# Relation stage of a four-layer graph network: three of four tiles turned by the transposing transfer, one of four by TensorE

## The chip, the core and the metric

The kernel runs on one core of a Trainium2 chip. A core has TensorE (PE: matrix products into PSUM, with its weight loads, PEld), VectorE (DVE), ScalarE (ACT), GpSimd (POOL) and SyncE (SP), which run in parallel, each through its own list of instructions in order, and meet at semaphores. DMAs are issued by SP, ACT and POOL and run on 16 shared DMA engines. The metric is the device time of one execution in microseconds.

## The reference

Four graph layers with a residual and a layer norm after each. The change lies in the last, a relational graph convolution followed by a plain one:

```python
def _graph_encoder(x, edge_index, edge_type, W_rel, W_root, b_rgcn, W_gcn, b_gcn):
    n = x.shape[0]
    src, dst = (edge_index[0], edge_index[1])
    ones = jnp.ones((src.shape[0],), dtype=x.dtype)
    seg = edge_type * n + dst
    agg = jax.ops.segment_sum(x[src], seg, num_segments=N_REL * n)
    cnt = jax.ops.segment_sum(ones, seg, num_segments=N_REL * n)
    mean = agg.reshape(N_REL, n, -1) / jnp.maximum(cnt, 1.0).reshape(N_REL, n, 1)
    h1 = jnp.einsum('rni,rio->no', mean, W_rel) + x @ W_root + b_rgcn
    ...
x = _layernorm(x + _L3_gnn_ref(x, edge_index, edge_type_34, ...), axis=-1)
```

There are 1250 nodes with 768 features, 20000 edges and 34 relations, each with its own 768 x 768 weights, all in 32-bit floating point.

## The kernel before

The layers run one after the other. In the relation stage the kernel doesn't form the means first. It has sorted the edges by relation and cut each relation's edges into tiles of 128, padded, `RT` = 190 tiles in all. For each tile it gathers the 128 source rows of x, multiplies them by the relation's weights, scales each row by the inverse count of its segment, and stores the messages to memory (`msg_d`). A later stage gathers and sums them by target node.

A product needs the tile turned: features on the partitions, edges along the row. There are two ways, and tiles with even and odd numbers take one each.

- **Turned by TensorE** (even tiles before). POOL gathers rows of `x3_d` into `rows7` (L1907). `turn` makes six transposes of 128 x 128 on TensorE into PSUM (L1936). `take` on ScalarE copies the result out of PSUM twice, plain into `xt7` (L1994) and rounded into `xhi7` (L1995).
- **Turned by a transfer** (odd tiles before; the code calls them crossed). POOL gathers rows of `x3p_d`, a copy of x in which each row is split in a plane of upper and one of lower 16-bit halves, into one of two buffers `halfs7`. `cross` on ScalarE's queue issues a transposing DMA from there into `plane7`, of which there is one (L1980). `take` puts the halves together into `xt7` (L1997) and rounds into `xhi7` (L1998).

After either, POOL subtracts the rounded from the plain values, `low` (L1913), so that the tile stands as a high and a low part. `messages` on TensorE is 36 matmuls (L1948): two halves of the 768 output columns, three products (high x high, high x low, low x high), six pieces of 128 features. Each tile's result takes two PSUM banks, and two tiles alternate. `store` on ScalarE scales the result into `msg7` (L2004) and issues its DMA (L2007). VectorE splits each relation's weights into high and low parts (L1880, L1881), and SyncE then loads the next relation's (L1873).

The order is written out by hand. For each tile k ScalarE does `store(k)`, then `take(k + 3)`, and after every second pair a `cross`. `store(k)` waits for the product of tile k, `take` for the turn or the transfer, and for `low` two tiles earlier. The product of tile k waits for `low(k)` and for `store(k - 2)`, which frees its PSUM. POOL issues the gather of an even tile when the one before it has been turned, and of a crossed tile when the transfer that read its buffer has landed; then it does `low(k)`.

Of the kernel before, what the change touches and what calls it, by code (L numbers as in the profile page):

```python
# [25 lines left out]
HALF = D // 2  # L26
# [3 lines left out]
RT = (E + R * (P - 1)) // P + 1  # L30
# [45 lines left out]
def build(nc, a, out):  # L76
    ctx = ExitStack()
    with ctx:
# [28 lines left out]
        ident = sb("ident", [P, P])  # L107
# [24 lines left out]
        ps = ctx.enter_context(nc.psum_tensor("ps", [P, 8, 512], F32))  # L132
# [25 lines left out]
        def halves(v):  # L158
            return v.rearrange("p (a n) -> p a n", a=2)
# [1725 lines left out]
        def dve_rel(v, step):  # L1885
# [12 lines left out]
                    relation(2 * i + 1 + u, 1 - u)  # L1898
            relation(R - 1, 1)

        def pool_rel(g, step):
            def gather(k):
                if k % 2 == 0 and k >= 2:
                    g.wait_ge(s_turn7, k // 2)
                if k % 2 == 1 and k >= 5:
                    g.wait_ge(s_cross7, 16 * ((k - 4) // 2 + 1))
                g.indirect_dma_start(out=rows7 if k % 2 == 0 else halfs7[:, k // 2 % 2, :], out_offset=None,  # L1907
                                     in_=x3_d if k % 2 == 0 else x3p_d,
                                     in_offset=bass.IndirectOffsetOnAxis(relrec[:, 2 * k:2 * k + 1], 0)).then_inc(s_gath[k % GW], 16)
# [6 lines left out]
            for k in (1, 0, 3):  # L1916
                gather(k)
            g.dma_start(rows8, row_d.rearrange("(p k) c -> p (k c)", p=P)).then_inc(s_idx8, 16)
            for k in range(RT):
                ahead = k + (2 if k % 2 == 0 else 4)  # L1920
                if ahead < RT:
                    gather(ahead)
                low(k)
            for u in range(GW):
                g.wait_ge(s_gath[u], 16 * len(range(u, RT, GW)))

        def pe_rel(pe):
            W_ROOT.multiply_resident(pe, lambda j: z6[:, j, :], lambda j: pe.wait_ge(s_ready6, j + 1))
            pe.sem_inc(s_prod7, 2)

            def turn(u, gathers, k):
                pe.wait_ge(s_gath[u % GW], 16 * gathers)
                if not isinstance(k, int) or k >= 4:
                    pe.wait_ge(s_take7, k - 3)
                for c in range(KC):
                    last = pe.transpose(ps[:, 2 * (u // 2 % 2) + c // 3, (c % 3) * P:(c % 3 + 1) * P], rows7[:, c * P:(c + 1) * P], ident[:, :])  # L1936
                last.then_inc(s_turn7, 1)

            def messages(k, u):
                r = pe.value_load(tile_rel[0:1, bass.ds(k, 1)], min_val=0, max_val=R - 1)  # L1940
                pe.wait_ge(s_split7, r + 2)
                base = (r % 2) * (KC * D)
                pe.wait_ge(s_lo7, k + 1)
                pe.wait_ge(s_emp7, k + 1)
                for h in range(2):
                    for q, (x, w) in enumerate(((xhi7, whi7), (xhi7, wlo7), (xlo7, whi7))):
                        for c in range(KC):
                            last = pe.matmul(ps[:, 4 + 2 * (u % 2) + h, 0:HALF], x[:, u, c * P:(c + 1) * P],  # L1948
                                             w[:, bass.ds(base + (c * D + h * HALF), HALF)],
                                             start=(q == 0 and c == 0), stop=(q == 2 and c == KC - 1))  # L1950
                last.then_inc(s_prod7, 1)

            turn(0, 1, 0)
            pe.wait_ge(W_ROOT.emptied, W_ROOT.b["emptied"] + NT + 2)
            turn(2, 1, 2)
            messages(0, 0)
            messages(1, 1)
            whole = (RT - 4) // XW
            with pe.Fori(0, whole) as i:
                for u in range(2, XW + 2):  # L1960
                    k = XW * i + u
                    if u % 2 == 0:
                        turn(u + 2, i + 1 + (u + 2) // XW, k + 2)
                    messages(k, u % XW)
            for k in range(whole * XW + 2, RT):
                if k % 2 == 0 and k + 2 < RT:
                    turn(k + 2, (k + 2) // XW + 1, k + 2)
                messages(k, k % XW)

        def act_rel(act, step):  # L1970
            act_root(act)
            act.wait_ge(W_ROOT.product, W_ROOT.all_products)

            def cross(u, gathers, taken=True):


                act.wait_ge(s_gath[u % GW], 16 * gathers)
                if taken:
                    act.sem_inc(s_take7, 1)
                act.dma_start_transpose(plane7.rearrange("p (c r) -> p c r", r=P), halfs7[:, u // 2 % 2, :]).then_inc(s_cross7, 16)  # L1980

            def take(k, u, turns):
                if u % 2 == 0:
                    act.wait_ge(s_turn7, turns)
# [6 lines left out]
                x = xt7[:, u % 2].rearrange("p c n -> p (c n)")  # L1991
                if u % 2 == 0:
                    pair = ps[:, 2 * (u // 2 % 2):2 * (u // 2 % 2) + 2, 0:HALF]
                    step.count(act.activation(halves(x), pair, ACT.Copy))  # L1994
                    step(act.activation(halves(xhi7[:, u % XW, :]), pair, ACT.Copy))  # L1995
                else:
                    step(act.activation(x.bitcast(U16).rearrange("p (n t) -> p t n", t=2), plane7.rearrange("p (t n) -> p t n", t=2), ACT.Copy))  # L1997
                    step(act.activation(xhi7[:, u % XW, :], x, ACT.Copy))  # L1998
                    act.sem_inc(s_take7, 1)  # L1999

            def store(k, u, stores):
                act.wait_ge(s_prod7, k + 3)
                act.wait_ge(s_msgst[u % 2], PLANES - 16 + 16 * stores)
                step(act.activation(halves(msg7[:, u % 2, :]), ps[:, 4 + 2 * (u % 2):6 + 2 * (u % 2), 0:HALF], ACT.Copy,  # L2004
                                    scale=invs[:, bass.ds(k, 1)]))
                act.sem_inc(s_emp7, 1)
                act.dma_start(msg_d[bass.ds(k * P, P), :], msg7[:, u % 2, :]).then_inc(s_msgst[u % 2], 16)  # L2007

            act.sem_inc(s_emp7, 2)
            cross(1, 1, taken=False)  # L2010
            take(0, 0, 1)
            act.sem_inc(s_take7, 1)
            take(1, 1, 1)
            take(2, 2, 2)
            cross(3, 1)
            store(0, 0, 1)
            take(3, 3, 2)
            store(1, 1, 1)
            take(4, 4, 3)
            cross(5, 2)  # L2020
            whole = (RT - 6) // XW
            with step.loop(whole, 3 * XW) as i:
                for u in range(XW):
                    k = XW * i + u + 2
                    store(k, u + 2, 2 * i + 1 + (u + 2) // 2)
# [3 lines left out]
            for k in range(whole * XW + 2, RT):  # L2029
                store(k, k, k // 2 + 1)  # L2030
                if k + 3 < RT:
                    take(k + 3, k + 3, (k + 3) // 2 + 1)
                    if k % 2 == 1:
                        cross(k + 4, (k + 4) // XW + 1)
            for u in range(2):
                act.wait_ge(s_msgst[u], PLANES - 16 + 16 * (RT // 2 + 1))


        UP = 4
# [216 lines left out]
```

## Time and profile before

| | us |
|---|---|
| median of 3 runs | 3793.22 (3791.40 to 3793.32) |
| the profiled execution, its own time | 3791.21 |
| its span in the profile | 3789.6 |
| mean granted clock of TensorE, share of full speed | 0.971 |

The span is what one profile shows from first to last instruction; the execution's own time lies 1.6 us above it. The relation stage's products run from 2074.8 to 3325.8 us, a third of the span. In the views, ACTq, POOLq and SPq are the queues in which ScalarE, POOL and SyncE issue DMAs; "idle before" is how long the engine did nothing before an instruction, and behind the arrow stands what ended it. The names of tiles are those of the buffers they are cut from: `ct` holds `rows7`, `halfs7`, `plane7`, `xt7` and `msg7`; `xsplit` holds `xhi7` and `xlo7`; `wsplit` the split weights; `ps` is PSUM.

### The profile page before, as it was taken

How to read it: one execution, taken by the hardware profiler on the slowest of the kernel's cores; microseconds unless marked ns; L12 is line 12 of the kernel's file. 1: busy time of each engine (PE TensorE's matmuls, PEld its weight loads, DVE VectorE, ACT ScalarE, POOL GpSimd, SP SyncE). 2: the span in 40 equal slices, each digit the busy share in tenths (PEclk: the TensorE clock that was granted, in tenths of full speed). 3: DMA queues.
4: the chain of work that ended last, by engine and by line, in shares of the span. 5: the costliest groups of instructions: out<-in, count | busy, mean ns of one | idle time of the engine just before them, and what ended most of it. 6: DMA issues, size and time to landing. Idle time of an engine off the chain costs nothing.

```text
span 3789.6 us, 56202 instructions
## 1 busy us (share of the span) xinstructions
PE 3509.1 (93%) x17647; PEld 2879.3 (76%) x17663; DVE 1956.8 (52%) x2740; ACT 1804.7 (48%) x2929; POOL 1751.0 (46%) x1329
## 2 busy tenths in 40 slices
PE   8998769999889897599989999999999999989998
PEld 4654449999789896233336999999999999955598
DVE  7537788888434545899955333333333331023335
ACT  1117878888633222599972444444444444400021
POOL 6888887765300001677101444444444444367600
PEclk9999979999989998899999999999999999999999
DMA  3321123333323213211025777777777775589801
GB/s 110 96 67 27 36 51 77 97 79 81 94 100 103 88 42 105 82 42 42 35 82 174 231 224 220 229 218 210 220 221 227 224 224 149 136 289 305 259 15 67
DMA packets 327199, 509.49 MB, mean 134 GB/s; under 512 B 195219, under 2 KB 211658, under 8 KB 327076
## 3 DMA queue, kind: packets, MB, share of 16 engines
q0 software_dynamic: 59584, 185.70, 16.9%
q1 hardware_dynamic: 85412, 194.37, 15.3%
q10 hardware_dynamic: 182080, 127.88, 12.0%
q8 instruction: 65, 1.06, 0.1%
q14 instruction: 58, 0.48, 0.0%
HBM read 346.22 MB, written 123.73 MB: 124 GB/s over the span
## 4 chain that ended last, share of the span: by engine, by line
PE 40%; ACT 7%; POOL 5%; issue 3%; DVE 2%; DMA 1%; SPq 0%; POOLq 0%; DVEq 0%; ACTq 0%
PE ps L1948 31%; POOL work L2055 5%; ACT work L1305 4%; ACT ps L1296 3%; PE ps L1588 3%; PE ps L307 2%; PE ps L1936 2%; PE ps L299 2%; DVE work L1127 1%; PE ps L1242 1%; DVE work L1155 0%; ACT work L1315 0%; DMA ct<-x_d 0%; DMA work<-msg_d,ct 0%; PE ps L325 0%
## 5 line engine op out<-in xcount | busy, mean ns | idle before, releaser
L1948 PE MATMUL ps<-wsplit,xsplit 128*128 x6840 | 1212.8, 336 | 0.0
L1948 PEld LDWEIGHTS ps<-wsplit,xsplit 128*128 128x128 f32 x6840 | 1185.0, 188 | 0.2 <-issue 0.2
L1913 POOL TENSOR_TENSOR xsplit<-ct,xsplit 128x768 fp32r<-128x768 f32 x190 | 361.4, 1902 | 368.6 <-ACTq L1999 240.8
L1305 ACT ACTIVATE work<-ps,work 128x418 f32<-128x418 f32 x720 | 438.4, 632 | 107.3 <-PE ps L1215 101.7
L1880 DVE CAST wsplit<-wplain 128x768 fp32r<-128x768 f32 x204 | 137.7, 675 | 680.1 <-PE ps L1948 659.2
L1252 PE MATMUL ps<-hbuf,work 128*128 128x193 f32 x2400 | 454.7, 327 | 16.2 <-DVE work L1169 13.1
L1252 PEld LDWEIGHTS ps<-hbuf,work 128*128 128x128 f32 x2400 | 407.0, 190 | 44.0 <-issue 16.7
L1296 ACT ACTIVATE ps<-work,lr 128x418 f32<-128x418 f32 x720 | 431.4, 633 | 6.4 <-DMA work<-lrow_d 6.4
L1155 DVE SCALAR_TENSOR_TENSOR work<-work,cnt 128x1250 f32<-128x1250 f32 x240 | 349.7, 1457 | 133.8 <-ACT work L1305 131.4
L2004 ACT ACTIVATE ct<-ps,invs 128x768 f32<-128x768 f32 x190 | 171.8, 904 | 485.7 <-PE ps L1948 472.6
L1242 PE MATMUL ps<-work,hbuf 128*65 128x512 f32 x720 | 323.4, 532 | 37.8 <-DVE work L1155 36.0
L299 PE MATMUL ps<-wsplit,xsplit 128*128 128x384 f32 x1800 | 336.7, 345 | 12.7 <-DVE xsplit L370 11.9
L299 PEld LDWEIGHTS ps<-wsplit,xsplit 128*128 128x128 f32 x1800 | 322.3, 195 | 15.0 <-issue 12.9
L801 POOL DMA_INDIRECT row_d<-hbuf x160 | 257.0, 1606 | 50.9 <-issue 48.5
L1215 PE MATMUL ps<-work 128*128 128x418 bf16 x720 | 247.4, 345 | 30.3 <-DMA work<-shift_d 25.9
L801 POOL DMA_INDIRECT relrec_d<-work x160 | 251.8, 1574 | 48.8 <-issue 48.5
L1349 POOL DMA_INDIRECT invs<-inv_d,relrec x190 | 219.6, 1156 | 117.5 <-issue 61.4
L2069 PE MATMUL ps<-work 128*128 128x384 f32 x784 | 257.2, 490 | 12.7 <-DMA work<-msg_d,ct 12.6
L1881 DVE TENSOR_TENSOR wsplit<-wplain,wsplit 128x768 fp32r<-128x768 f32 x204 | 253.8, 1244 | 7.1
L801 POOL DMA_INDIRECT dstrec_d<-work x160 | 216.7, 1354 | 66.5 <-issue 48.5
L2069 PEld LDWEIGHTS ps<-work 128*128 128x128 f32 x784 | 149.4, 191 | 120.1 <-issue 15.5
L1997 ACT ACTIVATE ct<-ct 128x1536 uint16<-128x1536 uint16 x95 | 186.1, 1959 | 111.8 <-DMA ct<-ct 65.8
(221 smaller groups left out, 4247.9 us busy)
## 6 DMA issues: line engine op xcount, KB each, us to landing
wplain<-in_L_gnn_W_rel SPq DMA_DIRECT2D x34, 2304.0 KB, 10.5
msg_d<-ct ACTq DMA_DIRECT2D x190, 384.0 KB, 2.6
work<-lrow_d SPq DMA_DIRECT2D x47, 625.0 KB, 3.9
feat_d<-work ACTq DMA_DIRECT2D x30, 386.0 KB, 2.6
hbuf<-feat_d SPq DMA_DIRECT2D x60, 193.0 KB, 2.5
gat_d<-work POOLq DMA_DIRECT2D x12, 960.0 KB, 5.3
xplain<-gat_d SPq DMA_DIRECT2D x30, 384.0 KB, 3.1
wplain<-x_d SPq DMA_DIRECT2D x20, 384.0 KB, 3.1
```

What stands on the lines that cost most here:

```text
L299: last = pe.matmul(ps[:, 4 + 2 * u + h, 0:HALF], x[:, u, c * P:(c + 1) * P], w[:, c * D + h * HALF:c * D + (h + 1) * HALF], start=(q == 0 ...
L801: g.indirect_dma_start(out=(dstrec_d, relrec_d, row_d)[which], out_offset=bass.IndirectOffsetOnAxis((addr[:, 1, t:t + 1], addr[:, 0, t:t + ...
L1155: v.scalar_tensor_tensor(p[:, 0:N], p[:, 0:N], 1.0, cnt3[:, q % NT, 0:N], ALU.min, ALU.mult).then_inc(self.s_p, 1)
L1215: pe.matmul(ps[:, b, 0:c1 - c0], self.ones128, self.crow[h % 2][:, c0:c1], start=False, stop=True, skip_group_check=True).then_inc(self.s_ ...
L1242: last = pe.matmul(ps[0:C + 1, 3 + k, 0:n1 - n0], self.feat(h, s), p[:, n0:n1], start=(s == 0), stop=(s == NT - 1))
L1252: last = pe.matmul(ps[:, self.b0 + b, t * (C + 1):(t + 1) * (C + 1)], p[:, dt * P:(dt + 1) * P], self.feat(h, s), start=(s == 0 and t == 0 ...
L1296: act.activation(ps[:, b, 0:c1 - c0], self.Rb[h % 2][:, c0:c1], ACT.Relu, bias=lr[:, col:col + 1]).then_inc(self.s_relu, 1)
L1305: act.activation(self.p[q % 3][:, c0:c1], ps[:, b, 0:c1 - c0], ACT.Exp, bias=self.l2[:, col:col + 1], scale=1.0 - SLOPE)\
L1881: step(v.tensor_tensor(wlo7[:, at:at + D], w, whi7[:, at:at + D].bitcast(F32), ALU.subtract))
L1913: g.tensor_tensor(xlo7[:, k % XW, :], xt7[:, k % 2].rearrange("p c n -> p (c n)"), xhi7[:, k % XW, :].bitcast(F32), ALU.subtract).then_inc ...
L1948: last = pe.matmul(ps[:, 4 + 2 * (u % 2) + h, 0:HALF], x[:, u, c * P:(c + 1) * P], w[:, bass.ds(base + (c * D + h * HALF), HALF)], start=( ...
L2069: last = pe.matmul(ps[:, 2 * (u % 2) + h, 0:HALF], sel8[:, GT * (u % 2) + w, :], mg8[:, GT * u + w, h * HALF:(h + 1) * HALF], start=(w == ...
```

## The change

Tiles with a number that four divides are turned by TensorE, all others by the transfer: 48 and 142 instead of 95 and 95. `crossed(k)` counts the crossed tiles below k, and so names the buffer of `halfs7` and the count of transfers to wait for. `cross` moves into `take`: as soon as a crossed tile is taken, the transfer for the next crossed tile is issued. ScalarE's loop body covers eight tiles instead of four. Turned tiles use one pair of PSUM banks instead of two in turn.

```diff
+        def by_transfer(k):
+            return k % XW != 0
+
+        def crossed(k):
+            return k - (k + XW - 1) // XW
+
+        def next_crossed(k):
+            return k + 1 if by_transfer(k + 1) else k + 2
...
             def gather(k):
-                if k % 2 == 0 and k >= 2:
-                    g.wait_ge(s_turn7, k // 2)
-                if k % 2 == 1 and k >= 5:
-                    g.wait_ge(s_cross7, 16 * ((k - 4) // 2 + 1))
-                g.indirect_dma_start(out=rows7 if k % 2 == 0 else halfs7[:, k // 2 % 2, :], out_offset=None,
-                                     in_=x3_d if k % 2 == 0 else x3p_d,
+                if by_transfer(k):
+                    if crossed(k) >= 2:
+                        g.wait_ge(s_cross7, 16 * (crossed(k) - 1))
+                    rows, source = halfs7[:, crossed(k) % 2, :], x3p_d
+                else:
+                    if k >= XW:
+                        g.wait_ge(s_turn7, k // XW)
+                    rows, source = rows7, x3_d
+                g.indirect_dma_start(out=rows, out_offset=None, in_=source,
...
-                ahead = k + (2 if k % 2 == 0 else 4)
+                ahead = next_crossed(next_crossed(k)) if by_transfer(k) else k + XW
...
-            turn(0, 1, 0)
+            turn(1, 0)
             pe.wait_ge(W_ROOT.emptied, W_ROOT.b["emptied"] + NT + 2)
-            turn(2, 1, 2)
-            messages(0, 0)
-            messages(1, 1)
+            for k in range(2):
+                messages(k, k)
             whole = (RT - 4) // XW
             with pe.Fori(0, whole) as i:
                 for u in range(2, XW + 2):
-                    k = XW * i + u
-                    if u % 2 == 0:
-                        turn(u + 2, i + 1 + (u + 2) // XW, k + 2)
-                    messages(k, u % XW)
+                    if u == 2:
+                        turn(i + 2, XW * i + XW)
+                    messages(XW * i + u, u % XW)
...
+            TURN = 2 * XW
...
-            def take(k, u, turns):
+            def take(i, c, more=True):
+                k = TURN * i + c
+                if by_transfer(c):
+                    act.wait_ge(s_cross7, 16 * (crossed(TURN) * i + crossed(c) + 1))
                 else:
-                    act.wait_ge(s_cross7, 16 * turns)
+                    act.wait_ge(s_turn7, 2 * i + c // XW + 1)
...
+                if by_transfer(c):
+                    step(act.activation(x.bitcast(U16).rearrange("p (n t) -> p t n", t=2), plane7.rearrange("p (t n) -> p t n", t=2), ACT.Copy))
+                    step(act.activation(xhi7[:, c % XW, :], x, ACT.Copy))
+                    if more:
+                        cross(i, next_crossed(c))
+                    else:
+                        act.sem_inc(s_take7, 1)
...
-                    take(k + 3, u + 5, 2 * i + (u + 5) // 2 + 1)
-                    if u % 2 == 1:
-                        cross(u + 6, i + (u + 6) // XW + 1)
+            whole = (RT - 6) // TURN - 1
+            with step.loop(whole, 3 * TURN) as i:
+                for c in range(2, TURN + 2):
+                    store(i, c)
+                    take(i, c + 3)
```

ScalarE's list before, just ahead of its loop, from the transfer for tile 3 to the transfer for tile 5. In brackets are the semaphores an instruction waits for: `product7` the product, `turned7` and `turned_by_transfer7` the two ways of turning, `rows_gathered` a gather, `act_step` ScalarE's own last instruction.

```order
L1980 DMA_TRANSPOSE ct<-ct 128x12x128 [waits act_step,rows_gathered3]
L2004 ACTIVATE ct<-ps,invs 128x768 [waits messages_stored0,product7]
L2007 DMA msg_d<-ct 128x768 [waits act_step]
L1997 ACTIVATE ct<-ct 128x2x768 [waits low_parts7,turned_by_transfer7]
L1998 ACTIVATE xsplit<-ct 128x768 [waits act_step]
L2004 ACTIVATE ct<-ps,invs 128x768 [waits act_step,messages_stored1,product7]
L2007 DMA msg_d<-ct 128x768 [waits act_step]
L1994 ACTIVATE ct<-ps 128x768 [waits product7,low_parts7,turned7]
L1995 ACTIVATE xsplit<-ps 128x768
L1980 DMA_TRANSPOSE ct<-ct 128x12x128 [waits act_step,rows_gathered1]
```

Between two transfers stand two stores and the takes of tile 3 and tile 4. ScalarE's list after, at the same place, from the transfer for tile 2 to the one for tile 5:

```order
L1993 DMA_TRANSPOSE ct<-ct 128x12x128 [waits act_step,rows_gathered2]
L2008 ACTIVATE ct<-ct 128x2x768 [waits low_parts7,turned_by_transfer7]
L2009 ACTIVATE xsplit<-ct 128x768 [waits act_step]
L1993 DMA_TRANSPOSE ct<-ct 128x12x128 [waits act_step,rows_gathered3]
L2024 ACTIVATE ct<-ps,invs 128x768 [waits messages_stored0,product7]
L2027 DMA msg_d<-ct 128x768 [waits act_step]
L2008 ACTIVATE ct<-ct 128x2x768 [waits low_parts7,turned_by_transfer7]
L2009 ACTIVATE xsplit<-ct 128x768 [waits act_step]
L1993 DMA_TRANSPOSE ct<-ct 128x12x128 [waits act_step,rows_gathered1]
```

A transfer now stands right behind each take of a crossed tile, and the next crossed tile's take waits for it with at most one store between. TensorE's list at the stage's start before: the turns (L1936) of tiles 0 and 2, then the first product's look-up of its relation.

```order
L307 MATMUL ps<-mask,ct 128x384 x24
L1936 MATMUL ps<-ident,ct 128x128 x12
L1940 TENSOR_LOAD tile_rel
L1940 ISA x2
L1941 REGISTER_ALU
```

The same place after, with `turn` now on L1949:

```order
L307 MATMUL ps<-mask,ct 128x384 x24
L1949 MATMUL ps<-ident,ct 128x128 x6
L1953 TENSOR_LOAD tile_rel
L1953 ISA x2
L1954 REGISTER_ALU
```

Tile 2's six transposes are gone from it.

## Rows read from the trace of the kernel before

**Rows 1.** The page: the span

```profile
span 3789.6 us, 56202 instructions
```

**Rows 2.** Chain of waits, 2500 to 2700 us: shares by line; start us, us, what

```profile
by line: PE ps L1948 95.2%; PE ps L1936 4.9%
...
2564.01 12.51 PE ps L1948 x72
2590.32 12.51 PE ps L1948 x72
```

**Rows 3.** Stretches: window, us, busy us of each engine, granted clock, DMA share, GB/s

```profile
3000.00:3200.00 200.00, 200.00 (x1187) 199.49 (x1186) 59.00 (x68) 92.84 (x92) 89.15 (x61) 1.00 0.68 198
```

**Rows 4.** Groups by line, 2100 to 3100 us: busy us, mean ns | idle before, releasers

```profile
L1997 ACT ACTIVATE ct<-ct 128x1536 uint16<-128x1536 uint16 x77 | 151.0, 1961 | 94.6 <-DMA ct<-ct 60.2 <-ACT ct L2004 34.4
L2004 ACT ACTIVATE ct<-ps,invs 128x768 f32<-128x768 f32 x152 | 137.4, 904 | 377.1 <-PE ps L1948 364.2 <-issue 7.6 <-ACT xsplit L1998 5.4
```

**Rows 5.** ScalarE's timeline: start us, us, engine, line, op [idle before, releaser]

```profile
2602.97 0.90 ACT L2004 ACTIVATE ct<-ps,invs 128x768 f32<-128x768 f32 x1 [1.53 <-PE ps L1948]
...
2604.67 0.82 ACT L1994 ACTIVATE ct<-ps 128x768 f32<-128x768 f32 x1 [0.80 <-ACT ct L2004]
2605.38 0.81 ACT L1995 ACTIVATE xsplit<-ps 128x768 fp32r<-128x768 f32 x1
2606.37 1.83 ACTq L1980 DMA_TRANSPOSE ct<-ct  x1
2609.95 0.90 ACT L2004 ACTIVATE ct<-ps,invs 128x768 f32<-128x768 f32 x1 [3.76 <-PE ps L1948]
2611.11 0.35 ACTq L2007 DMA_DIRECT2D msg_d<-ct  x1
2611.66 1.97 ACT L1997 ACTIVATE ct<-ct 128x1536 uint16<-128x1536 uint16 x1 [0.81 <-ACT ct L2004]
2613.67 0.85 ACT L1998 ACTIVATE xsplit<-ct 128x768 fp32r<-128x768 f32 x1
2616.11 0.90 ACT L2004 ACTIVATE ct<-ps,invs 128x768 f32<-128x768 f32 x1 [1.59 <-PE ps L1948]
...
2619.50 2.88 ACTq L1980 DMA_TRANSPOSE ct<-ct  x1
...
2626.71 1.95 ACT L1997 ACTIVATE ct<-ct 128x1536 uint16<-128x1536 uint16 x1 [2.66 <-DMA ct<-ct]
...
2629.88 0.90 ACT L2004 ACTIVATE ct<-ps,invs 128x768 f32<-128x768 f32 x1 [0.34 <-ACT xsplit L1998]
```

**Rows 6.** Timeline of all engines, same columns

```profile
2602.67 0.82 PE L1936 MATMUL ps<-ident,ct 128*128 128x128 f32 x6
...
2614.64 0.37 SPq L1873 DMA_DIRECT2D wplain<-in_L_gnn_W_rel  x1
```

**Rows 7.** Line L1980, 2100 to 3300 us: duration ns min/median/max, landing

```profile
L1980 ACTq DMA_TRANSPOSE ct<-ct x91: 1452/2032/4160, 2106.4 to 3290.5; - x91
...
DMA to landing us min/median/max: 3.7/4.3/8.2
```

**Rows 8.** DMA issues, 2100 to 3100 us: xcount, KB each, median us to landing

```profile
wplain<-in_L_gnn_W_rel SPq DMA_DIRECT2D x30, 2304.0 KB, 10.5
msg_d<-ct ACTq DMA_DIRECT2D x152, 384.0 KB, 2.6
...
ct<-x3p_d,relrec POOLq DMA_INDIRECT x76, 4.5
```

**Rows 9.** ScalarE's timeline at the stage's start

```profile
2076.68 5.49 ACTq L1980 DMA_TRANSPOSE ct<-ct  x1
...
2087.53 1.98 ACT L1997 ACTIVATE ct<-ct 128x1536 uint16<-128x1536 uint16 x1 [3.12 <-DMA ct<-ct]
```

**Rows 10.** TensorE's timeline near 3600 us

```profile
3600.58 6.24 PE L299 MATMUL ps<-wsplit,xsplit 128*128 128x384 f32 x24 [2.23 <-DVE xsplit L370]
```

**Rows 11.** Stretches: the columns of rows 3, after that wait

```profile
3601.80:3605.20 3.40, 3.37 (x11) 3.31 (x11) 3.04 (x4) 0.00 (x0) 0.00 (x0) 0.51 0.06 25
```

More of the change, by code:

```diff
@@ L1914, in low @@
                                 ALU.subtract).then_inc(s_lo7, 1)
-            for k in (1, 0, 3):
+            for k in (1, 0, 2):
                 gather(k)
@@ L1929, in pe_rel, with turn @@
             pe.sem_inc(s_prod7, 2)
[L1931 to L1934, printed above, removed]
+            def turn(gathers, k):
+                pe.wait_ge(s_gath[0], 16 * gathers)
+                if not isinstance(k, int) or k >= XW:
+                    pe.wait_ge(s_take7, k - XW + 1)
                 for c in range(KC):
-                    last = pe.transpose(ps[:, 2 * (u // 2 % 2) + c // 3, (c % 3) * P:(c % 3 + 1) * P], rows7[:, c * P:(c + 1) * P], ident[:, :])
+                    last = pe.transpose(ps[:, c // 3, (c % 3) * P:(c % 3 + 1) * P], rows7[:, c * P:(c + 1) * P], ident[:, :])
                 last.then_inc(s_turn7, 1)
@@ L1960, in pe_rel @@
                 for u in range(2, XW + 2):
-                    k = XW * i + u
-                    if u % 2 == 0:
-                        turn(u + 2, i + 1 + (u + 2) // XW, k + 2)
-                    messages(k, u % XW)
+                    if u == 2:
+                        turn(i + 2, XW * i + XW)
+                    messages(XW * i + u, u % XW)
             for k in range(whole * XW + 2, RT):
-                if k % 2 == 0 and k + 2 < RT:
-                    turn(k + 2, (k + 2) // XW + 1, k + 2)
+                if not by_transfer(k + 2) and k + 2 < RT:
+                    turn((k + 2) // XW + 1, k + 2)
                 messages(k, k % XW)
@@ L1972, in act_rel, with cross @@
             act.wait_ge(W_ROOT.product, W_ROOT.all_products)
-            def cross(u, gathers, taken=True):
-                act.wait_ge(s_gath[u % GW], 16 * gathers)
+            TURN = 2 * XW
+            def cross(i, c, taken=True):
+                act.wait_ge(s_gath[c % GW], 16 * (2 * i + c // XW + 1))
                 if taken:
                     act.sem_inc(s_take7, 1)
-                act.dma_start_transpose(plane7.rearrange("p (c r) -> p c r", r=P), halfs7[:, u // 2 % 2, :]).then_inc(s_cross7, 16)
-            def take(k, u, turns):
-                if u % 2 == 0:
-                    act.wait_ge(s_turn7, turns)
+                act.dma_start_transpose(plane7.rearrange("p (c r) -> p c r", r=P), halfs7[:, crossed(c) % 2, :]).then_inc(s_cross7, 16)
+            def take(i, c, more=True):
+                k = TURN * i + c
+                if by_transfer(c):
+                    act.wait_ge(s_cross7, 16 * (crossed(TURN) * i + crossed(c) + 1))
                 else:
-                    act.wait_ge(s_cross7, 16 * turns)
+                    act.wait_ge(s_turn7, 2 * i + c // XW + 1)
                 if not isinstance(k, int) or k >= 2:
@@ L1990, in take @@
                     act.wait_ge(s_prod7, k - 1)
[L1991 to L1993 removed]
+                x = xt7[:, c % 2].rearrange("p c n -> p (c n)")
+                if by_transfer(c):
[5 more added lines that the diff above has]
+                        act.sem_inc(s_take7, 1)
+                else:
+                    pair = ps[:, 0:2, 0:HALF]
@@ L1994, in take, with store @@
                     step.count(act.activation(halves(x), pair, ACT.Copy))
[L1995 to L1998, printed above, removed]
+                    step(act.activation(halves(xhi7[:, c % XW, :]), pair, ACT.Copy))
                     act.sem_inc(s_take7, 1)
-            def store(k, u, stores):
+            def store(i, c):
+                k, u = TURN * i + c, c % 2
@@ L2002, in store @@
                 act.wait_ge(s_prod7, k + 3)
-                act.wait_ge(s_msgst[u % 2], PLANES - 16 + 16 * stores)
-                step(act.activation(halves(msg7[:, u % 2, :]), ps[:, 4 + 2 * (u % 2):6 + 2 * (u % 2), 0:HALF], ACT.Copy,
+                act.wait_ge(s_msgst[u], PLANES + 16 * ((TURN // 2) * i + c // 2))
+                step(act.activation(halves(msg7[:, u, :]), ps[:, 4 + 2 * u:6 + 2 * u, 0:HALF], ACT.Copy,
                                     scale=invs[:, bass.ds(k, 1)]))
                 act.sem_inc(s_emp7, 1)
-                act.dma_start(msg_d[bass.ds(k * P, P), :], msg7[:, u % 2, :]).then_inc(s_msgst[u % 2], 16)
+                act.dma_start(msg_d[bass.ds(k * P, P), :], msg7[:, u, :]).then_inc(s_msgst[u], 16)
@@ L2009, in act_rel @@
             act.sem_inc(s_emp7, 2)
[L2010 to L2025, printed above, removed]
-                    take(k + 3, u + 5, 2 * i + (u + 5) // 2 + 1)
-                    if u % 2 == 1:
-                        cross(u + 6, i + (u + 6) // XW + 1)
@@ L2029, in act_rel @@
-            for k in range(whole * XW + 2, RT):
-                store(k, k, k // 2 + 1)
+            cross(0, 1, taken=False)
+            for k in range(3):
+                take(0, k)
+            for k in range(2):
+                store(0, k)
+                take(0, k + 3)
+            whole = (RT - 6) // TURN - 1
[3 more added lines that the diff above has]
+                    take(i, c + 3)
+            for k in range(whole * TURN + 2, RT):
+                store(0, k)
@@ L2031, in act_rel @@
                 if k + 3 < RT:
-                    take(k + 3, k + 3, (k + 3) // 2 + 1)
-                    if k % 2 == 1:
-                        cross(k + 4, (k + 4) // XW + 1)
+                    take(0, k + 3, next_crossed(k + 3) < RT)
             for u in range(2):
-                act.wait_ge(s_msgst[u], PLANES - 16 + 16 * (RT // 2 + 1))
+                act.wait_ge(s_msgst[u], PLANES + 16 * (RT // 2))
         UP = 4
```

## Prediction

> **What bounds the kernel now.** I read the span first, 3789.6 us [rows 1], and then the chain of waits over the relation stage, where the change is. There the chain is TensorE (PE) alone: 95.2% message products (L1948) and 4.9% turns (L1936) [rows 2]. The table by stretches agrees: PE busy 200.00 of 200 us at granted clock 1.00, ScalarE (ACT) only 92.84 [rows 3]. So in this stage every microsecond off TensorE's list is one off the run, as long as nobody arrives late. Who could be late, the groups by line [rows 4] and ScalarE's timeline [rows 5, 6] tell: of 1000 us ScalarE waits 364.2 for a product to end, and 60.2 for a transposing transfer to land. That second wait is the one to watch.
>
> **What the change removes.** A message product is 36 matmuls. Four tiles take 26.31 us (2564.01 to 2590.32); their two pairs of products are 2 x 12.51 = 25.02 of it [rows 2]. The two turns between them cost the rest, 1.29, or 0.65 us each. (A turn's six transposes are busy for 0.82 us [rows 6], but overlap the products, so I take 0.65.) Of 190 tiles, 95 are turned on TensorE before and 48, every fourth, after: 47 x 0.65 = **-30.6 us**. TensorE's floor for four tiles becomes 25.02 + 0.65 = 25.67 us. This is the whole gain, and it needs the transfers to keep up.
>
> **What it adds.** 47 more transfers, and above all a new order: for three tiles of four ScalarE's list is store, take, transfer, and the next tile's take waits for exactly that transfer. There is one buffer for turned planes (`plane7`), so a transfer can't be issued before the take that empties it has ended. Before, a tile turned by TensorE lay between any two takes from `plane7`, and the transfer had that time. ScalarE's steps:
> - Store to the take after it, when nothing is waited for: 2609.95 to 2611.66, 1.71 us [rows 5].
> - A take from a transfer, up to the issue of the next: from 2611.66 to the end of the second ACTIVATE at 2614.52, and the 0.18 that lie between the end of L1995 (2606.19) and the issue at 2606.37: 3.04 us [rows 5].
> - The issue holds ScalarE's sequencer for a median of 2.03 us (1.45 to 4.16) [rows 7]; all that is queued behind it on ScalarE waits. About 0.3 more to the next store.
> - Issue to landing: median 4.3 us (3.7 to 8.2) [rows 7], and 0.2 to the take.
> - A take from TensorE's turn: 2604.67 to 2606.19, 1.52 us, and 0.34 to a store that follows a take at once (2629.88) [rows 5].
>
> From one transferred tile's take to the next: 3.04 + 4.5 = 7.5 us, where a tile's products are 12.51 / 2 = 6.25. ScalarE falls behind by 1.3 us at each of the two steps of a group that go from transfer to transfer. In the third the turned tile lies between, and the transfer is hidden: 3.04 + 2.03 + 0.3 + 1.71 + 1.52 + 0.34 + 1.71 = 10.7. A group of four: 2 x 7.5 + 10.7 = **25.7 us**, against TensorE's 25.67. Undisturbed, ScalarE just keeps pace (47 groups x 0.03, **+2**) and can catch nothing up. From the shortest values of [rows 7] the group is 2 x 6.9 + 10.1 = 23.9 and ScalarE gains 1.8 us in each; if every issue held it for 2.88, as the one at 2619.50 did, the steps would be 3.04 + 2.88 + 0.3 + 1.71 = 7.9 and the group 27.4, 1.7 us late each time (+80 us). I take the medians, since they come from 91 transfers.
>
> How late may ScalarE be? A store frees the PSUM that the product two tiles on writes. The one at 2609.95 is done at 2610.85. That product starts some 0.3 us before the store at 2616.11, as PE's turn at 2602.67 stands before the store at 2602.97: 2615.8 - 2610.9 = 4.9 us of cover [rows 5, 6]. Behind a late take on ScalarE stands the next store, for which TensorE waits, and POOL's low part with the gather after it.
>
> **The weight loads.** Every fifth tile, on average, SyncE loads 2304 KB, 10.5 us from issue to landing, 30 times in 1000 us [rows 8]. The transfer issued 4.9 us into such a load (2614.64, 2619.50) gave its take at 2626.71, 7.2 us later instead of 4.5, and ScalarE stood idle for it [rows 5, 6]: +2.7. Before, this lay inside the cover. Afterwards three transfers are issued in 25.7 us; if those issued in the first 7 us of a load are hit, a load meets 3 x 7 / 25.7 = 0.8 of them (an estimate), 25 in some 31 loads. One third is hidden behind the turned tile and costs only the longer hold, 2.88 - 2.03 = 0.85: 8 x 0.85 = 7. The others cost 2.7 each: 17 x 2.7 = 46. Together **+53 us**, and **-5** for the cover, which is used up once because nothing is caught up. Bounds: nothing (first rival), and 25 x 3.9 = 98 us with the longest landing, 8.2.
>
> **The start.** Tile 2 now also comes by transfer, in the middle of the first weight load. Before, the transfer issued at 2076.68 held ScalarE for 5.49 us and gave its take at 2087.53 [rows 9]. TensorE has one turn less ahead of the first product (0.65), and may then wait for tile 2 until that landing plus the take: between -1 and +6, I take **+3**. POOL's gathers of crossed tiles are issued when a transfer lands and are needed two transfers later, some 10 us on; they land after 4.5 [rows 8] and cost nothing. Without that cover each late gather would delay a transfer by its lateness.
>
> **Sum**, on the profiled execution's 3791.2 us (span 3789.6 and what lies around it): -30.6 + 2 + 53 - 5 + 3 = +22, 3813 us. The median of the runs, 3793.2, lies 2 higher; between the two I say **3814 us**.
>
> Two statements of the Trainium skill would make it come out better. "Advanced Engine Details and Errata", section X-Bar Transpose (TRN2), calls transposing DMAs as fast as regular ones. Here a plain store of 384 KB lands after 2.6 us [rows 8], a transfer of as many bytes after 4.3 [rows 7]: the trace disagrees. With 2.6, ScalarE's own 2.03 + 0.3 + 1.71 would bound the step, 7.1, and the group would be 24.9 us. "DMA: Bandwidth & Descriptors", section Issuing engines are not separate DMA queues, calls the sequencer's time to start a DMA usually small beside the DMA. Here it is 2.03 of 4.3 us [rows 7]; with the 0.35 of a store [rows 5] the group would be 24.0, which is the first rival.
>
> **Rivals.**
> - *The cover holds (faster).* The same two takes per group, but transfers at nearly their shortest values. The weight loads cost 53 / 31 = 1.7 us per five tiles, 1.4 per group; from a group of 25.67 - 1.4 = 24.3 us on ScalarE makes that up again, and TensorE never waits: 3791.2 - 30.6 + 3 = 3764 us. For it: 23.9 is within the spread of [rows 7], and of 1000 us ScalarE now has 364 to spare [rows 4]. Against it: the medians.
> - *Stalls cool TensorE (slower still).* Each hit would be a wait of 2 to 4 us at TensorE. The wait of 2.23 us ahead of 3600.58 was followed by 3.4 us at granted clock 0.51, 1.2 instead of 2.4 GHz [rows 10, 11]. 3.4 us at half rate cost 1.7; 17 times, 29, of which some lets ScalarE catch up: 3814 + 25 = 3839 us. Against it: a stall spread over two tiles stays shorter.
> - *Nothing to see.* Half of the hits fall where they are covered: -30.6 + 2 + 27 + 3 = +1, some 3793 us. The wait would only have moved from the turns to ScalarE.
>
> **Chances.** A measurement of this kernel tells about 0.2% (7.6 us) from no change. Forecast, with its own range 3803 to 3832: 0.42. Cooling, 3825 to 3860: 0.20. The cover holds, 3760 to 3784: 0.24. Nothing to see: 0.14. So slower 0.62, same 0.14, faster 0.24. The range leaves out about a tenth at each side: 3770 to 3852.
>
> **What would show it.** Turns: 48 x 6 transposes at TensorE. The chain of waits in the stage should no longer be TensorE alone but pass through ScalarE's takes and stores and the transfer; TensorE should be busy for less than 100% of the stage, with waits of 1 to 4 us after weight loads, released by ScalarE's store. ScalarE's waits for a product should shrink from 364 us in 1000 to under 100, those for a transfer double. I am wrong if ScalarE still waits for a product before most stores (the first rival), if the transfers' median landing is under 3.9 us or over 5, or if a gather or the weights release TensorE's waits.

## The result and the profile after

The changed kernel takes **3861.3 us** (median of 4 runs, 3860.16 to 3866.08), the one before 3793.2: a ratio of 1.0183, 95% interval 1.0163 to 1.0203. A fourth run of the kernel before, of 5027.1 us, was a slow one and is left out. The change makes the kernel slower by 68 us, and the time lies 9 us above the predicted range. The profiled execution took 3860.2 us.

The first view is the chain of waits of the changed kernel over 2500 to 2800 us of the relation stage (start us, us, what).

```profile
by line: DMA ct<-ct 42.5%; ACT ct L2008 21.7%; ACT xsplit L2009 9.4%; issue 6.7%; ACTq L1993 5.8%; ACT ct L2024 4.9%; ACT xsplit L2017 2.7%; ACTq L2027 2.3%; POOL xsplit L1926 1.9%; ACTq L1992 0.3%; ACTq L69 0.3%; ACT ct L2016 0.3%; ACTq L1
...
2506.89 3.67 DMA ct<-ct
...
2520.31 13.77 DMA ct<-ct
...
2586.85 8.96 DMA ct<-ct
...
2616.02 3.69 DMA ct<-ct
...
2622.71 10.14 DMA ct<-ct
```

In [rows 2] the chain was TensorE alone. Now TensorE isn't in it: it runs from transfer (`ct<-ct`) to take (L2008, L2009) to the issue of the next transfer (L1993). Most links through a transfer are 3.7 us long, and some are 6 to 14.

The table by stretches answers to [rows 3] (same columns): TensorE, which was never idle, is busy for 1036.57 of 1100 us.

```profile
2100.00:3200.00 1100.00, 1036.57 (x5883) 1020.74 (x5883) 374.65 (x372) 533.17 (x473) 473.84 (x316) 0.98 0.78 223
```

The groups by line, 2100 to 3100 us, answer to [rows 4]; the two rows behind them are from the view of waits (engine, line, waited for: us in all, times, longest).

```profile
L1961 PE MATMUL ps<-wsplit,xsplit 128*128 x5131 | 923.5, 339 | 59.6 <-ACTq L2026 58.2 <-issue 1.0
...
L2008 ACT ACTIVATE ct<-ct 128x1536 uint16<-128x1536 uint16 x107 | 209.9, 1962 | 173.9 <-DMA ct<-ct 148.5 <-POOL xsplit L1926 18.8 <-ACT ct L2024 6.6
...
L2024 ACT ACTIVATE ct<-ps,invs 128x768 f32<-128x768 f32 x143 | 129.2, 904 | 315.0 <-issue 201.6 <-PE ps L1961 96.2 <-ACT xsplit L2017 17.2
```

```profile
ACT ct L2008 <- DMA ct<-ct: 148.5, 76, 10.8
...
PE ps L1961 <- ACTq L2026: 58.2, 32, 7.2
```

L2026 is the semaphore that ScalarE raises when a store (L2024) has emptied its PSUM. It is the only thing of weight for which the products wait: 32 waits, 1.8 us on average. ScalarE's waits for a product fell from 364.2 to 96.2 us; its waits for a transfer rose from 60.2 to 148.5.

The view of the transfer's line answers to [rows 7], and the DMA issues, 2100 to 3100 us, to [rows 8].

```profile
L1993 ACTq DMA_TRANSPOSE ct<-ct x139: 1306/1468/6511, 2098.7 to 3367.5; - x139
...
DMA to landing us min/median/max: 3.6/3.7/17.8
```

```profile
wplain<-in_L_gnn_W_rel SPq DMA_DIRECT2D x28, 2304.0 KB, 10.4
msg_d<-ct ACTq DMA_DIRECT2D x143, 384.0 KB, 3.5
```

The median transfer became faster (landing 3.7 instead of 4.3 us, ScalarE's sequencer held for 1.47 instead of 2.03), while the worst became far slower: 17.8 us instead of 8.2, with a hold of 6.51 instead of 4.16.

Where the slow ones are, the timeline shows (columns as in [rows 5]; SPq L1873 is the weight load):

```profile
2616.02 1.46 ACTq L1993 DMA_TRANSPOSE ct<-ct  x1
...
2619.74 1.96 ACT L2008 ACTIVATE ct<-ct 128x1536 uint16<-128x1536 uint16 x1 [1.08 <-DMA ct<-ct]
2621.20 37.38 SPq L1873 DMA_DIRECT2D wplain<-in_L_gnn_W_rel  x2
...
2622.71 5.35 ACTq L1993 DMA_TRANSPOSE ct<-ct  x1
...
2628.35 0.90 ACT L2024 ACTIVATE ct<-ps,invs 128x768 f32<-128x768 f32 x1 [5.78 <-PE ps L1961]
...
2629.60 6.52 PE L1961 MATMUL ps<-wsplit,xsplit 128*128 x36 [1.34 <-ACTq L2026]
...
2632.86 1.95 ACT L2008 ACTIVATE ct<-ct 128x1536 uint16<-128x1536 uint16 x1 [3.61 <-DMA ct<-ct]
...
2635.88 1.48 ACTq L1993 DMA_TRANSPOSE ct<-ct  x1
...
2638.87 18.99 PE L1961 MATMUL ps<-wsplit,xsplit 128*128 x108 [2.75 <-ACTq L2026]
```

The transfer at 2616.02 gave its take 3.7 us later. A weight load was issued at 2621.20 (the row joins it with the next one, hence its length), and the transfer 1.5 us behind it held ScalarE for 5.35 us, gave its take after 10.1, and left TensorE waiting twice, for 1.34 and 2.75 us. The wait of 5.78 ahead of the store bears the name of the product, but ScalarE's sequencer was held by the issue in that time; the product had long ended, as TensorE's own wait shows. Over the whole stage the DMA packets of 142 transfers show 108 done on average 3.24 us after their issue, and 34 past 4.5 us, 9.04 on average, that is 5.8 later. I call these 34 the hits. Each of the 33 loads issued in the stage has one, and one load has two.

What happens inside such a hit is seen in the DMA packets that start in each half microsecond. A transfer of 384 KB is moved in packets of 256 bytes (1536 of them), a load in packets of 3072 (768).

```
                 load's packets   transfer's packets
no load:
2515.0 to 2515.5        0              423
2515.5 to 2516.0        0              417
transfer issued at 2520.31, load at 2519.92:
2525.5 to 2526.0       64               64
2526.5 to 2527.0       40               43
2528.0 to 2528.5       30               30
2530.5 to 2531.0       38               96
2532.5 to 2533.0        4              235
2533.0 to 2533.5        0              348
```

While the load runs, the transfer gets about one small packet for each large one at first, two to three late in the load, and full speed only when the load's packets end. In the hits done after 7 us or more, two thirds of the transfer's packets on average start when nearly all (98%) of the load's have started. The Trainium skill has the rule in "DMA: Bandwidth & Descriptors", section Queues, rings and completion order: each DMA engine takes turns between the queues that have work, packet by packet. The equal counts up to 2528.5 agree with it; the later rows, with more small packets than large, aren't explained by it alone.

### The profile page after: what moved, and what is told of

Same layout as the page of the kernel before. It is cut to its first block, busy times and chain, and to the rows that moved or that the text cites. A ratio compares the mean times of both kernels' runs of the same rounds, so it can differ in the third digit from the quotient of the medians.

```text
span 3858.6 us, 55480 instructions
## 1 busy us (share of the span) xinstructions
PE 3510.3 (91%) x17365; PEld 2860.0 (74%) x17381; DVE 1970.8 (51%) x2740; ACT 1865.4 (48%) x2929; POOL 1769.6 (46%) x1329
## 4 chain that ended last, share of the span: by engine, by line
ACT 17%; PE 15%; DMA 13%; POOL 5%; issue 5%; ACTq 3%; DVE 2%; SPq 0%; POOLq 0%; DVEq 0%
DMA ct<-ct 12%; PE ps L1961 8%; ACT ct L2008 5%; POOL work L2065 5%; ACT work L1305 4%; ACT ps L1296 3%; PE ps L1588 3%; ACT xsplit L2009 2%; PE ps L307 2%; ACTq L1993 2%; PE ps L299 1%; ACT ct L2024 1%; DVE work L1127 1%; ACT xsplit L2017 1%; PE ps L1242 1%
## 5 line engine op out<-in xcount | busy, mean ns | idle before, releaser
L1961 PE MATMUL ps<-wsplit,xsplit 128*128 x6840 | 1227.7, 339 | 70.2 <-ACTq L2026 63.3
L1880 DVE CAST wsplit<-wplain 128x768 fp32r<-128x768 f32 x204 | 169.8, 832 | 733.9 <-PE ps L1961 699.2
L2008 ACT ACTIVATE ct<-ct 128x1536 uint16<-128x1536 uint16 x142 | 278.4, 1960 | 224.6 <-DMA ct<-ct 190.9
L2024 ACT ACTIVATE ct<-ps,invs 128x768 f32<-128x768 f32 x190 | 171.7, 904 | 414.4 <-issue 238.3
L1921 POOL DMA_INDIRECT ct<-x3p_d,relrec x142 | 149.9, 1056 | 336.8 <-DMA ct<-ct 322.7
L1881 DVE TENSOR_TENSOR wsplit<-wplain,wsplit 128x768 fp32r<-128x768 f32 x204 | 236.7, 1160 | 7.1
```

## The experiments

The theory after the result: each weight load holds up one transfer of the chain for most of the load's own length, because the two are issued at nearly the same time, and nothing else is late. The rivals: ScalarE's chain is too slow by itself; the DMA engines have too little rate in all (a rate that the loads merely share), wherever in time the loads lie; a gather or POOL is late; the cooled TensorE is the main loss. All ratios are to the kernel before on the same chip, with 95% intervals. Since the layers ahead of the stage alone differ by up to 12 us from profile to profile, I also give the products' stretch, from the start of the first product to that of the last: 1250.6 us before, 1314.9 after.

**Loads all but left out, after and before.**

```diff
-                sp.dma_start(w, rel[bass.ds(i + 1, 1)].rearrange("r p c n -> (r p) c n")).then_inc(s_wrel, 16)
+                sp.dma_start(w[:, 0:1, 0:64], rel[bass.ds(i + 1, 1)].rearrange("r p c n -> (r p) c n")[:, 0:1, 0:64]).then_inc(s_wrel, 16)
```

> The changed kernel with the weight loads of relations 1 to 33 cut to 64 columns of one of six pieces (24 to 32 KB instead of 2304 KB), so all relations but the first compute with stale weights. Theory A (each weight load stalls one transfer of ScalarE's chain, and nothing else is late): the turns saved remain, less some 4 us at the start: 3793 - 31 + 4 = 3766 us, TensorE busy for 100% of the relation stage from 2200 us on, transfers landing after 3.7 us with none over 5. Theory B (store, take and transfer in a row are too slow by themselves, whatever else runs): still above 3830 us, TensorE waits in the stage. Theory C (the change at the start costs most): near 3850, waits only in the first 50 us.

> Control: the kernel before with the same cut of the weight loads (stale weights for all relations but the first). Theories A, B and C: TensorE bounds the stage and no load is waited for, so 3793 us, within 0.2%; if it falls by more, the loads cost the kernel before as well (by DMA traffic or by VectorE's splits) and the gain of the other run must be read against this one.

The changed kernel: 3753.0 us, 0.9901 (0.9880 to 0.9922). The kernel before: 3789.3, 1.0001 (0.9986 to 1.0017). The transfer's line and the stretch in the changed kernel without loads:

```profile
L1993 ACTq DMA_TRANSPOSE ct<-ct x139: 1292/1464/2407, 2101.8 to 3278.1; - x139
...
DMA to landing us min/median/max: 3.6/3.7/4.4
```

```profile
2100.00:3200.00 1100.00, 1100.00 (x6437) 1098.55 (x6436) 374.60 (x394) 583.70 (x517) 515.22 (x345) 1.00 0.65 170
```

No transfer in these rows lands later than 4.4 us, TensorE is never idle, and its clock is full throughout. The products' stretch is 1220.0 us long, 1250.6 in the kernel before with its loads: the 30.6 us of the turns, to the tenth. So neither ScalarE's chain by itself nor a gather costs anything, and the loads cost the kernel before nothing that can be measured (its stretch without them is 1249.6). They cost the changed one 94.9 us of stretch (1314.9 - 1220.0). The medians give 108 (3861.3 - 3753.0); of that some 13 lie outside the stretch, where runs of one kernel differ as much: the four runs without loads span 3750.9 to 3767.6, the profiled one being the slowest. Theory A had expected 3766.

**Half of each load left out** (three of six pieces).

```diff
-                sp.dma_start(w, rel[bass.ds(i + 1, 1)].rearrange("r p c n -> (r p) c n")).then_inc(s_wrel, 16)
+                sp.dma_start(w[:, 0:3], rel[bass.ds(i + 1, 1)].rearrange("r p c n -> (r p) c n")[:, 0:3]).then_inc(s_wrel, 16)
```

> The changed kernel with half of each weight load left out (1152 instead of 2304 KB; three of six pieces keep stale weights from relation 1 on), issued at the same place in one DMA. Theory A, with the landing of a transfer that meets a load set by the packets queued ahead and beside it: half the packets, so the hit landings fall from about 9.5 us to about 6.5, most of which the cover holds: 3765 to 3800 us. If a hit costs a fixed amount, whatever the load's size: near 3860.

3795.8 us, 1.0009 (0.9990 to 1.0027), as Theory A had it.

```profile
2100.00:3200.00 1100.00, 1081.90 (x6261) 1074.52 (x6260) 391.95 (x394) 567.46 (x503) 509.40 (x335) 0.99 0.74 199
```

The cost of the loads in the stretch is 30 us with half of each (1250.1) and 95 with the whole: it grows faster than the load's length. That fits a first part of each hit that is covered; an estimate of it stands below the table.

**Each load in six DMAs of 384 KB**, each issued as soon as VectorE has split that piece, 1.6 to 3.3 us apart.

```diff
...
             with sp.Fori(0, R - 1) as i:
-                sp.wait_ge(s_split7, i + 2)
-                sp.dma_start(w, rel[bass.ds(i + 1, 1)].rearrange("r p c n -> (r p) c n")).then_inc(s_wrel, 16)
+                for c in range(KC):
+                    sp.wait_ge(s_split7, i * KC + c + 2)
+                    sp.dma_start(w[:, c], rel[bass.ds(i + 1, 1)].rearrange("r p c n -> (r p) c n")[:, c]).then_inc(s_wrel, 16)
...
```

Not shown: the first relation's load is cut in six as well, VectorE counts each piece that it has split, and the waits count pieces.

> The changed kernel with each weight load cut into six DMAs of 384 KB, each issued as soon as VectorE has split the piece that it replaces, so that a load is spread over the 12 us of the splits and never has 2304 KB queued. All results are computed. Theory A: a transfer meets one piece of 384 KB at most, so its landing rises by 1 to 3 us instead of up to 14 and most of the rise lies inside the 4.9 us of cover: 3766 to 3785 us, below the kernel before. If it is the amount of bytes and not the queue ahead of the transfer that delays it: near 3860 as the changed kernel. Theory B: near 3860. Theory C: near 3860.

> Control: the kernel before with the same loads in six pieces, all results computed. TensorE bounds the stage, so 3793 us within 0.2% by every theory; a rise would mean that the six smaller loads or their semaphore counts cost time of their own.

The changed kernel: 3820.5 us, 1.0074 (1.0051 to 1.0098). The kernel before: 3817.6, 1.0057 (1.0027 to 1.0086). Theory A's 3766 to 3785 didn't come, nor did the control's 3793. The control tells most here, since the six pieces made the kernel before lose 24 us, 19 of them in the products' stretch (1270.0). Its takes (L1998) and its products (L1949), 2100 to 3200 us:

```profile
L1949 PE MATMUL ps<-wsplit,xsplit 128*128 x5915 | 1054.4, 337 | 12.4 <-POOL xsplit L1914 12.3
...
L1998 ACT ACTIVATE ct<-ct 128x1536 uint16<-128x1536 uint16 x82 | 160.9, 1962 | 215.2 <-DMA ct<-ct 210.1 <-ACT ct L2005 5.1
```

The take now waits 210.1 us for transfers, where [rows 4] has 60.2 in 1000 us. The pieces are small, but they are issued one behind the other for some 10 us, and a transfer that meets this train waits for it as it does for one load: the longest landing was 13.9 us. So cutting a load isn't enough: this points to how long load packets are there without a break. Behind a late take POOL's low part is late, and TensorE waits 12.3 us for it. The changed kernel gained by the pieces (transfers up to 12.9 us instead of 17.8), but is still slower than the kernel before and no faster than its control.

**Each load in three DMAs of 768 KB, issued just behind three stores.** ScalarE's semaphore after a store releases a piece (VectorE, between its splits, waits for it and passes it on), some 3.6 us before the next transfer (8 where a second store lies between), so that much of the piece is through when the transfer is issued, and the rest is short.

```diff
...
-                sp.wait_ge(s_split7, i + 2)
-                sp.dma_start(w, rel[bass.ds(i + 1, 1)].rearrange("r p c n -> (r p) c n")).then_inc(s_wrel, 16)
+                for j in range(3):
+                    sp.wait_ge(s_ready6, i * 3 + NT + j + 1)
+                    sp.dma_start(w[:, 2 * j:2 * j + 2], rel[bass.ds(i + 1, 1)].rearrange("r p c n -> (r p) c n")[:, 2 * j:2 * j + 2]).then_inc(s_wrel, 16)
...
                 for c in range(KC):
                     split7(v, step, u, c)
+                    if c % 2 == 1:
+                        v.wait_ge(s_emp7, last + 4 + c // 2)
+                        v.sem_inc(s_ready6, 1)
```

Not shown: the counts for the first relation, and VectorE's wait for three DMAs instead of one.

> The changed kernel with each weight load cut into three DMAs of 768 KB, each issued when ScalarE has just stored a tile (the counter that the store raises), about 3.6 us before the next transfer is issued, in three tiles following each other. All results are computed. Theory A (a transfer is held up by the weight packets that stand or run beside it, and ScalarE's chain has no other trouble): the 768 KB have gone by when the transfer starts, landings stay at 3.7 to 5 us, TensorE waits for less than 10 us in the stage after its first 100 us: 3753 to 3775 us, faster than the kernel before by 0.5 to 1%. Theory D (the bytes slow the stage wherever they stand, as 20 of the 33 us lost with six pieces suggest): about 3820 as with six pieces.

> Control: the kernel before with the same three DMAs at the same counter, all results computed. Theory A: no transfer meets a load, TensorE bounds the stage, 3793 us within 0.2% (its own gain of avoided hits is nothing, since they lay inside the cover). Theory D: 3800 or more, as with six pieces (3818).

The changed kernel: **3758.4 us, 0.9912 (0.9893 to 0.9932)**. The kernel before: 3790.0, 0.9994 (0.9980 to 1.0007). The same bytes are moved and the DMA engines are busier than in the changed kernel (0.82 against 0.78), yet TensorE is never idle and its clock is full:

```profile
2100.00:3200.00 1100.00, 1100.00 (x6438) 1098.51 (x6437) 319.20 (x398) 581.82 (x516) 521.60 (x345) 1.00 0.82 237
```

```profile
L1998 ACTq DMA_TRANSPOSE ct<-ct x138: 1305/1665/2615, 2102.0 to 3268.2; - x138
...
DMA to landing us min/median/max: 3.6/4.2/7.1
```

So it isn't the rate in all. The median landing is even longer than in the changed kernel, 4.2 against 3.7 us; what is gone is the tail. That the change's own gain is whole again shows against the control: 3758.4 - 3790.0 = -31.6 us, and 1219.0 - 1249.3 = -30.3 in the stretch. This version is faster than both kernels.

**The whole load in one DMA, behind a store.** Is it the moment or the pieces that helped?

```diff
...
-                sp.wait_ge(s_split7, i + 2)
+                sp.wait_ge(s_ready6, i + NT + 1)
                 sp.dma_start(w, rel[bass.ds(i + 1, 1)].rearrange("r p c n -> (r p) c n")).then_inc(s_wrel, 16)
...
                 for c in range(KC):
                     split7(v, step, u, c)
+                v.wait_ge(s_emp7, last + 5)
+                v.sem_inc(s_ready6, 1)
```

> The changed kernel with each weight load whole (2304 KB in one DMA), but issued at the same counter as the paced version, when ScalarE has just stored a tile, so 3.6 us before the next transfer is issued. All results are computed. It tells place from size: if only the phase of the load against the transfer matters, near the paced version; theory A with queued packets: each load still meets a transfer 3 to 4 us after its issue, which lands after some 8 us, so one hit in each load with a loss of about 3 to 4 us instead of 5 to 6: 3815 to 3850 us.

3811.5 us, 1.0058 (1.0041 to 1.0075), a little under the 3815 to 3850 of theory A. The transfer's line, then the products, 2100 to 3200 us:

```profile
L1997 ACTq DMA_TRANSPOSE ct<-ct x135: 1306/1471/5053, 2103.3 to 3292.9; - x135
...
DMA to landing us min/median/max: 3.6/3.7/10.3
```

```profile
L1965 PE MATMUL ps<-wsplit,xsplit 128*128 x5898 | 1047.1, 337 | 33.7 <-ACTq L2030 32.6 <-issue 0.5
```

The moment alone nearly halves what the loads cost in the stretch (51 us instead of 95): transfers are now issued 3.5 us or more into a load, the longest landing falls from 17.8 to 10.3 us, and TensorE waits 32.6 us for stores. The rest of the gain needs the smaller pieces as well.

| kernel | us | ratio | longest landing, us | products' stretch, us |
|---|---|---|---|---|
| after | 3861.3 | 1.0183 | 17.8 | 1314.9 |
| after, half of each load left out | 3795.8 | 1.0009 | 15.9 | 1250.1 |
| after, six pieces in a train | 3820.5 | 1.0074 | 12.9 | 1272.0 |
| after, one load behind a store | 3811.5 | 1.0058 | 10.3 | 1271.4 |
| after, three pieces behind stores | 3758.4 | 0.9912 | 7.1 | 1219.0 |
| after, loads all but left out | 3753.0 | 0.9901 | 4.4 | 1220.0 |

How much of a hit is covered can be estimated from the DMA packets of these runs. If the first 3 us by which a transfer is late cost nothing, what lies beyond adds up to 102 us in the changed kernel (34 hits), 40 with half loads (24), 59 with one load behind a store (33) and 5 in the kernel before (18 hits, 2.9 us late on average). The stretches are longer than without loads by 95, 30, 51 and 1. The trains of six pieces don't fit it (25 against 52), and no run shows why.

## Why the prediction was wrong

The direction and the mechanism were right: slower, through ScalarE's takes and stores and the transfer, with waits of TensorE behind weight loads. The size was not: +22 was forecast, +68 measured. By its steps:

- **Turns, -30.6.** Right: the stretch of products without loads is shorter by just that, and the paced pair differs by 31.6.
- **ScalarE's chain, 25.7 us a group.** Wrong in value, inside its bounds. In the timeline of the changed kernel, undisturbed steps take 6.7 us from transfer to transfer (2645.81, 2652.50, 2659.26) and 10.4 with the turned tile between (2605.61, 2616.02): 2 x 6.7 + 10.4 = 23.8, what the shortest values of [rows 7] gave (23.9). The higher medians of before weren't due to loads: the run of the kernel before without them still has 1.93 for the hold and 4.2 for the landing. There POOL's gather moves 240 KB (median) from 0.5 to 3.5 us after a transfer's issue, and in the changed kernel without loads next to nothing; whether that is the cause no run tests. So ScalarE could win back some 1.8 us a group, and the term of +2 was none.
- **The weight loads, "The others cost 2.7 each: 17 x 2.7 = 46".** This step failed, in size and in count: 34 hits of 5.8 us on average, some 198 us in all, not 25 with 17 counted at 2.7. I took the 2.7 us from a transfer issued 4.9 us into a load [rows 5, 6], when nearly half of the load was through, and I spread the transfers evenly over the load.

  They aren't spread, neither before nor after. VectorE's split waits for a product (631.0 of 1000 us after the change), the load for the split, and the transfers follow takes and stores, which the products time as well; so the order of the work sets the phase. Before, 30 of the 33 loads had a transfer 4.9 to 5.1 or 10.1 us into them, in turn: nearly every price that I could read there was for a late phase. After the change 25 of the 34 hit transfers were issued between 0.8 us ahead of their load and 1.6 behind it, and had nearly the whole of it to wait for.

  It isn't the hits that pull them together: with the loads all but left out, 23 of the 33 loads still have a transfer issued between 0.8 us ahead and 1.2 behind, as here (the columns of [rows 5]):

```profile
2547.42 1.45 ACTq L1993 DMA_TRANSPOSE ct<-ct  x1
2548.24 0.33 SPq L1873 DMA_DIRECT2D wplain<-in_L_gnn_W_rel  x1
...
2579.42 0.33 SPq L1873 DMA_DIRECT2D wplain<-in_L_gnn_W_rel  x1
2579.90 1.54 ACTq L1993 DMA_TRANSPOSE ct<-ct  x1
```

  Even my upper bound, 25 x 3.9 = 98, was worked out from a single longest landing of a kernel in which the phase lay otherwise; that the loads' cost of 95 us lies just under it is luck.
- **The cover, -5, "used up once because nothing is caught up".** Wrong as well, and to the other side. At 23.8 us a group ScalarE wins back 1.8 to 1.9 us, some 2.7 between two loads (an estimate: 190 tiles, 33 loads), near the 3 us of each hit that cost nothing. So of 198 us of lateness only 95 came through to the stretch.
- **The start, +3.** Not borne out. The products begin at 2078.8 instead of 2074.8 us, but the stage's first turn, ahead of which nothing was changed, began at 2072.55 instead of 2067.39 in this profile (and at 2066.93 in that of the changed kernel with one load behind a store). From that turn to the first product it is 6.2 us instead of 7.4, in four other profiles of the changed kernel too, so the start gave -1.2. The take at 2089.08 then waited 9.69 us for a transfer issued behind the first load; it is one of the hits.
- **The rival "the cover holds"** had its condition fulfilled, a group under 24.3 us (23.8), and still didn't come: its point was worked out from hits of 53 us in all, not 198. With the loads paced it came to within 6 us of its 3764.
- **The rival "stalls cool TensorE"** was true in part and I had left it out of the likeliest case. At ten of the 14 waits of TensorE over 1.8 us the granted clock falls to 1.2 GHz, during the wait or within 1.6 us behind it, for 3.4 us or twice that, 44 us in all; before, there was none past the first 5 us of the products. An example is the wait of 7.16 us:

```profile
2122.67 7.66 PE L1961 MATMUL ps<-wsplit,xsplit 128*128 x34 [7.16 <-ACTq L2026]
```

```profile
2110.00:2130.00 20.00, 12.84 (x66) 12.53 (x64) 12.19 (x12) 7.36 (x6) 6.46 (x4) 0.83 0.75 194
```

A mean of 0.83 over 20 us is 6.8 us at half clock. About half of these lay inside the wait and cost nothing; the rest cost some 1.6 us. Over the products' stretch TensorE was busy for 41 us at half clock, which cost some 20, and 5 of these us before, 3. So the stretch, longer by 64.3 us, is made up of -30.6 (turns) + 65 (waits between products) + 18 (clock) = +52, and some 12 that this count doesn't place, about 0.35 us for each wait. The waits are the 70.2 us of the row below less the 5.39 ahead of the first product. The other 4 of the 68 us lie ahead of the stretch, where the layers before the stage took longer in this profile.

```profile
L1961 PE MATMUL ps<-wsplit,xsplit 128*128 x6840 | 1227.7, 339 | 70.2 <-ACTq L2026 63.3
```

This split between waiting and clock is read from the trace; no run holds the clock up while the waits stay. A sign that I had named was there: the median landing under 3.9 us. It told that the group was mispriced, not that the mechanism was wrong.

Not tried: a second `plane7`, which would let a transfer be issued before the take ahead of it. Whether SBUF has room for it, no run shows.

## What to carry to other kernels

Before a long-latency step is put into the chain that sets the time, ask for each large transfer in the stage when it is issued relative to that step after the change, not before: where the same engine's work times both, their phase is fixed, and the worst phase can be the usual one, not the mean. A trace shows this before any change is made: look whether the gap between the two issues repeats. Price the hit by the length of the large transfer, take off what the chain can win back between two hits, and look at the longest landing, not the median. If the mechanism is a collision in time, moving and cutting the large transfer can be worth more than the change itself: here three pieces behind stores turned +1.8% into -0.9%.

## What the runs showed of the hardware

- A transposing transfer of 384 KB with no load beside it lands in 3.6 to 4.4 us (changed kernel, loads all but left out); one issued just ahead of or behind a load of 2304 KB took up to 17.8, and it held the issuing engine's sequencer for up to 6.51 us. So the load reached the stores, which have nothing to do with the transfer but stand behind its issue.
- Six DMAs of 384 KB issued 1.6 to 3.3 us apart let transfers land only after up to 12.9 us (13.9 in the kernel before), against 17.8 beside one DMA of 2304 KB; with three of 768 KB, most of them 4 to 7.5 us apart, the longest landing was 7.1, although the DMA engines were busier.
